# Carry stationary, weights moving: a two-way row scan with its product turned by VectorE

## What is computed

```
v = (x - mean) / sqrt(var + 1e-5)          # per image and group of 32 channels
step(carry, row): new = relu(Wm @ carry + bias) + row      # Wm: 1024 x 1024, row: 1024 x (4*48)
down = scan(step, first row of v, the rows below it)
up   = scan(step, last row of down, the rows of down above it)
out  = x + up
```

## Time and profile before

| | |
|---|---|
| median of 3 runs | 1852.66 us (1851.65 to 1884.84) |
| span of the profiled execution | 1849.8 us |
| mean granted TensorE clock | 0.999 of 2.4 GHz |
| PE busy | 1717.1 us (93%) |
| DVE busy | 1197.4 us (65%) |
| POOL busy | 646.1 us (35%) |
| ACT busy | 316.9 us (17%) |

### The profile page before, as it was taken

The page is one execution under the profiler, slowest core; times in us unless marked ns, Lnnn a source line. Parts: engine busy times, 40 slices in busy tenths (PEclk is TensorE's granted clock), DMA queues, the critical chain, the costliest instruction groups (busy, mean ns, idle before and its releaser), DMA issues.

```text
span 1849.8 us, 33139 instructions
## 1 busy us (share of the span) xinstructions
PE 1717.1 (93%) x12036; PEld 1716.1 (93%) x12036; DVE 1197.4 (65%) x3282; ACT 316.9 (17%) x763; POOL 646.1 (35%) x1145
## 2 busy tenths in 40 slices
PE   0029999999999999999999999999999999999999
PEld 0029999999999999999999999999999999999999
DVE  7998666666666666666665666556565656566564
ACT  0011111111111111111111111111111111111111
POOL 0046444445444444444432222222222222222222
PEclk9999999999999999999999999999999999999999
DMA  9953222121212222220002242424333333424111
GB/s 352 368 188 120 95 76 102 68 103 68 102 68 103 76 94 87 83 97 23 0 0 78 110 153 102 153 102 154 115 140 124 132 134 122 147 108 153 51 51 51
DMA packets 61436, 206.07 MB, mean 111 GB/s; under 512 B 4160, under 2 KB 33856, under 8 KB 61376
## 3 DMA queue, kind: packets, MB, share of 16 engines
q1 hardware_dynamic: 61232, 205.54, 30.9%
q10 hardware_dynamic: 144, 0.00, 0.0%
HBM read 136.32 MB, written 69.21 MB: 111 GB/s over the span
## 4 chain that ended last, share of the span: by engine, by line
PE 91%; DMA 4%; DVE 4%; SPq 1%; issue 0%; ACT 0%; POOLq 0%; POOL 0%; DVEq 0%
PE bank L411 63%; PE bank L413 28%; DMA x_ring<-x_rows 2%; DMA d_ring<-x_rows 2%; DVE work L286 1%; SPq L142 1%; DVE d_ring L342 1%; DVE moments L297 0%; DVE carry L332 0%; DVE carry L334 0%; DVE w_lo L349 0%; DVE d_ring L365 0%; DVE summed L360 0%; DVE spread L311 0%; ACT work L273 0%
## 5 line engine op out<-in xcount | busy, mean ns | idle before, releaser
L411 PE MATMUL bank<-carry,w_hi 128*128 128x384 f32 x6016 | 1715.6, 360 | 13.2 <-DVE carry L334 10.0
L413 PE MATMUL bank<-carry,w_lo 128*128 128x192 f32 x6016 | 1507.6, 251 | 0.0
L413 PEld LDWEIGHTS bank<-carry,w_lo 128*128 128x128 f32 x6016 | 1151.2, 191 | 0.0
L411 PEld LDWEIGHTS bank<-carry,w_hi 128*128 128x128 f32 x6016 | 1131.1, 188 | 13.9 <-issue 9.9
L360 DVE TENSOR_TENSOR summed<-bank,work 128x192 f32<-128x192 f32 x752 | 267.0, 355 | 552.6 <-ACT work L273 531.9
L273 ACT ACTIVATE work<-bank,bias_sb 128x192 f32<-128x192 f32 x752 | 307.4, 421 | 1416.2 <-PE bank L413 1416.2
L243 POOL TENSOR_TENSOR x_ring<-x_ring,d_ring 128x192 f32<-128x192 f32 x384 | 228.8, 596 | 662.6 <-DVE carry L334 649.9
L334 DVE TENSOR_TENSOR carry<-d_ring,carry 128x192 fp32r<-128x192 f32 x752 | 337.7, 449 | 26.2
L223 POOL TENSOR_TENSOR xn<-x_ring,gn_mean 128x192 f32<-128x192 f32 x376 | 214.9, 572 | 396.2 <-DVE d_ring L365 387.1
L332 DVE CAST carry<-d_ring 128x192 fp32r<-128x192 f32 x752 | 197.2, 262 | 26.1
L226 POOL TENSOR_TENSOR xn<-xn,gn_rstd 128x192 f32<-128x192 f32 x376 | 191.5, 509 | 29.5
(11 more groups left out here) (24 smaller groups left out, 12.2 us busy)
## 6 DMA issues: line engine op xcount, KB each, us to landing
x_ring<-x_rows SPq DMA_DIRECT2D x88, 768.0 KB, 6.9
out_rows<-x_ring SPq DMA_DIRECT2D x47, 768.0 KB, 3.9
down_rows<-d_ring SPq DMA_DIRECT2D x40, 768.0 KB, 3.6
d_ring<-down_rows SPq DMA_DIRECT2D x40, 768.0 KB, 5.7
d_ring<-x_rows SPq DMA_DIRECT2D x12, 1536.0 KB, 16.2
x_ring<-x_rows SPq DMA_DIRECT2D x8, 1536.0 KB, 16.4
d_ring<-w_t SPq DMA_DIRECT2D x7, 512.0 KB, 8.9
out_rows<-x_ring SPq DMA_DIRECT2D x8, 96.0 KB, 1.6
```

The source lines that it names most:

```text
L411: pe.matmul(bank[m][:, 0:2 * COLS], w_hi[:, k, out_cols], carry[:, parity, k, :, :].rearrange("p s c -> p (s c)"), start=(k == 0), stop=False)
L413: last = pe.matmul(bank[m][:, 0:COLS], w_lo[:, k, out_cols], carry[:, parity, k, 0, :], start=False, stop=(k == K - 1))
```

## The change

The operands change places: 128 columns of the carry are the stationary operand, and 512 columns of the weights (half of the output channels) are the moving one. A row of 192 columns (4 images by 48) is cut into three chunks of 64 columns (4 images by 16). The three chunks are independent chains. A "step" `i` is now one chunk of one row, 282 in all (3 chunks, 94 rows). Job `j` computes one half of the output channels, half `j % 2`, for the two steps `j-1` and `j`, whose 64 columns each lie side by side as 128 stationary columns. So a step gets one of its halves in job `i` and the other in job `i+1`. There are 283 jobs; the first and the last have one step. Each has 24 matmuls of 512 columns, into one bank (8 tiles `k`, three part products).

The product now stands in PSUM with the carry's columns on the partitions and the output channels along a row, and it has to be turned before it can be the next carry. DVE does this with 16 transposes a job (`turn_blocks`, L442): each reads 32 partitions (quadrant `q`) by 128 elements of the bank and writes 32 partitions (quadrant `u`) of the buffer `turn`. The weights' output channels are laid out by the host so that this gives whole tiles. After the 16th, `direct_done` is raised; ACT does four activations in place (relu with bias, L341), raises `rectified`, and DVE makes two halves of rows from it (L457: product plus row, 128 by 256 elements each). ACT rounds each half to `st_hi` (L347), and POOL takes the remainder to `st_lo` (L289). Job `j` reads, in its first 12 matmuls, halves that job `j-3` completed, and in its last 12 also the half that job `j-2` completed.

```
-            def product(parity, m, k):
-                pe.matmul(bank[m][:, 0:2 * COLS], w_hi[:, k, out_cols], carry[...hi and lo...])
-                pe.matmul(bank[m][:, 0:COLS], w_lo[:, k, out_cols], carry[:, parity, k, 0, :])
+            for j in range(JOBS):
+                if j >= BANKS:
+                    pe.wait_ge(direct_done, j - BANKS + 1)
+                for n in range(K):
+                    k = KB * blocks_of(j)[n // KB] + n % KB
+                    wait_split(hi_ready, first_hi, j, n)
+                    pe.matmul(out, stationary(st_hi, j, k), w_cols(w_hi, o, k), ...)
+                    pe.matmul(out, stationary(st_hi, j, k), w_cols(w_lo, o, k), ...)
+                    wait_split(lo_ready, first_lo, j, n)
+                    last = pe.matmul(out, stationary(st_lo, j, k), w_cols(w_hi, o, k), ...)
+                    if final:
+                        last.then_inc(acc_ready, 1)
+            def turn_blocks(j):
+                dve.wait_ge(acc_ready, j + 1)
+                if j >= 2:
+                    dve.wait_ge(y_ready, first_done(j - 2))
+                for u in range(QUADS):
+                    for q in range(used(j) // B32):
+                        final = dve.transpose(target(j, q, u), source(bank[j % BANKS], q, u))
+                final.then_inc(direct_done, 1)
+            def make_half(j, i):
+                ... waits for xn_ready and d_stored (down) or d_loaded (up) ...
+                dve.tensor_tensor(here, product_of(j, i), addend, ALU.add).then_inc(y_ready, 1)
+            for j in range(JOBS):
+                turn_blocks(j)
+                dve.wait_ge(rectified, j + 1)
+                for i in members(j):
+                    make_half(j, i)
+            def rectify(j):                                     # ACT
+                act.wait_ge(direct_done, j + 1)
+                for kk in range(KB):
+                    cols = channels[j % 2][:, kk, 0:used(j)]
+                    final = act.activation(cols, cols, ACT.Relu, bias=bias_sb[:, k:k + 1])
+                final.then_inc(rectified, 1)
```

More of the change, by code:

```diff
@@ L26, with row_of, blocks_of, first_done @@
 P = 128
-SLOTS = 8
+K = 8
+KB = 4
+C = 1024
+H = 48
+NI = 4
+WIDTH = 48
+COLS = NI * WIDTH
+CHUNKS = 3
+W16 = WIDTH // CHUNKS
+Q = 64
+HALF = 512
+B32 = 32
+QUADS = 4
 GN_GROUP = 32
 GN_EPS = 1e-5
+BN_DIM = 6
+RING = 8
+GROUPS = H // RING
+LAST = GROUPS - 1
 STAT_CHUNKS = 4
-DVE_LO = 3
-WAVE = 5
-BN_DIM = 6
-def build(nc, x_rows, w_t, bias, down_rows, out_rows):
[L37 to L48, removed]
+TC = K // STAT_CHUNKS
+ROWS = H - 1
+STEPS = CHUNKS * ROWS * 2
+DOWN = CHUNKS * ROWS
+JOBS = STEPS + 1
+XN_SLOTS = 4
+BANKS = 8
+W_TILES = 16
+W_POOL = 13
+XN_AHEAD = 2
+SLOT_AT = ((0, 0), (0, 1), (P, 1), (P, 0))
+PAIR_AT = ((0, 2), (0, 1), (1, 2), (P, 1))
+def row_of(i):
+    step = i // CHUNKS
+    return step + 1 if step < ROWS else 2 * ROWS - 1 - step
+def blocks_of(j):
+    return ((j + 1) % 2, j % 2)
+def first_done(i):
+    return 2 * i + 1
+def second_done(i):
+    return 2 * i + 2
+def members(j):
+    return [i for i in (j - 1, j) if 0 <= i < STEPS]
+def build(nc, x_rows, w_t, bias, down_rows, out_rows):
     with ExitStack() as ctx:
@@ L58, in build @@
         w_lo = sb("w_lo", [P, K, C], F32R)
[L59 to L64, removed]
+        st_hi = sb("st_hi", [P, K, 2 * P], F32R)
+        st_lo = sb("st_lo", [P, K, 2 * P], F32R)
+        x_ring = sb("x_ring", [P, RING, K * COLS])
+        d_ring = sb("d_ring", [P, RING, K * COLS])
+        xn = sb("xn", [P, XN_SLOTS, K * Q])
+        turn = sb("turn", [P, 3 * HALF])
         bias_sb = sb("bias_sb", [P, K])
@@ new lines, in build, with w_place, w_order, w_cols @@
+        w_raw = [raw_area[:, t * HALF:(t + 1) * HALF] for t in range(W_TILES)]
+        def w_place(t):
+            o, n = divmod(t, K)
+            return o, KB * blocks_of(o)[n // KB] + n % KB
+        def w_order(o, k):
+            b = blocks_of(o).index(k // KB)
+            return K * o + KB * b + k % KB
+        def w_cols(w, o, k):
+            return w[:, k, o * HALF:(o + 1) * HALF]
+        def stat_cols(ring, i):
+            return ring[:, :, i * WIDTH:(i + 1) * WIDTH]
+        def x_chunk(h, c, k0=0, k1=K):
+            row = x_ring[:, h % RING, :].rearrange("p (k n w) -> p k n w", k=K, n=NI)
+            return row[:, k0:k1, :, c * W16:(c + 1) * W16]
@@ L165, in _ @@
[L165 to L200, removed]
@@ L228, in _ @@
[L228 to L243, removed]
-                                       ALU.add).then_inc(out_ready, 1)
@@ L268, in _ @@
-            act.wait_ge(bias_loaded, 16)
-            with act.Fori(0, STEPS) as s:
-                for m in range(K):
-                    act.wait_ge(psum_ready, K * s + m + 1)
-                    act.activation(act_part[:, m, :], bank[m][:, COLS:2 * COLS], ACT.Identity,
-                                   bias=bias_sb[:, m:m + 1]).then_inc(act_ready, 1)
+            act.activation(gn_std[:, :], bank[7][:, 0:K * NI], ACT.Sqrt, bias=eps[:, 0:1]).then_inc(std_ready, 1)
+            for t in range(3, K):
+                w_round(t)
@@ new lines, in split_hi @@
+            def split_hi(j, i):
+                b = j % 2
+                act.wait_ge(y_ready, first_done(i) if i == j else second_done(i))
+                act.activation(slot(st_hi, i + CHUNKS, b * KB, (b + 1) * KB),
+                               d_chunk(row_of(i), i % CHUNKS, b * KB, (b + 1) * KB), ACT.Copy).then_inc(hi_ready, 1)
+            for j in range(JOBS):
+                rectify(j)
+                for i in members(j):
+                    if i < STEPS - CHUNKS:
+                        split_hi(j, i)
@@ new lines, in wait_split @@
+            def wait_split(ready, first, j, n):
+                if j == 0 and n in (0, KB):
+                    pe.wait_ge(first, 1 + n // KB)
+                elif j in (1, 2) and n == 0:
+                    pe.wait_ge(first, 2 + j)
+                elif j >= CHUNKS and j < STEPS:
+                    if n == 0:
+                        pe.wait_ge(ready, first_done(j - CHUNKS))
+                    elif n == KB:
+                        pe.wait_ge(ready, second_done(j - CHUNKS))
+            for j in range(JOBS):
+                o = j % 2
+                out = bank[j % BANKS][0:used(j), :]
+                if j >= BANKS:
+                    pe.wait_ge(direct_done, j - BANKS + 1)
+                for n in range(K):
+                    k = KB * blocks_of(j)[n // KB] + n % KB
+                    final = n == K - 1
+                    wait_split(hi_ready, first_hi, j, n)
+                    if j < 2:
+                        wait_w(w_hi_ready, None, o, k)
+                    pe.matmul(out, stationary(st_hi, j, k), w_cols(w_hi, o, k), start=(n == 0), stop=False)
+                    if j < 2:
+                        wait_w(w_lo_ready, w_lo_rest_ready, o, k)
+                    pe.matmul(out, stationary(st_hi, j, k), w_cols(w_lo, o, k), start=False, stop=False)
+                    wait_split(lo_ready, first_lo, j, n)
+                    last = pe.matmul(out, stationary(st_lo, j, k), w_cols(w_hi, o, k), start=False, stop=final)
+                    if final:
+                        last.then_inc(acc_ready, 1)
```

363 lines of the change are left out of this document (184 added, 179 removed).

## The result

The changed kernel takes 2217.88 us (median of 4 runs, 2217.83 to 2218.11), and is slower by 19.75%: the ratio is 1.1975, 95% interval 1.1954 to 1.1996. Two of the runs of before taken beside it were disturbed (1885 us); the ratio leaves them out. The forecast was 2253 us.

What follows compares the result with a forecast made beforehand. PE bounded the kernel before; DVE was to bound the changed one: 281 cycles of 7.50 us plus 142.4 us for the ends make 2250, with 2.9 from profiled span to median 2253 us; range 1815 to 2480.

Steps and rivals of the forecast that it cites:

- PE's side: PE's matmuls: 5.12 to 5.66 us a job, 1449 to 1602 us for all 283, a gain on offer of 114 to 267.
- The sum of DVE: DVE's cycle for a job, a plain sum of transposes, wait for ACT and additions: 7.50 us.
- 16 transposes: DVE's transposes in each job: 0.28 + 0.043 = 0.324 us each, 5.18 us for 16.
- hand to ACT, four activations, hand back: DVE's wait for ACT in each job: 0.05 us there, 1.2 for four activations (1.14 raised), 0.04 back.
- two additions: DVE's additions of 256 elements each, priced from L334 beside POOL: 0.515 us each, 1.03 for two.
- case C: The forecast case, DVE-bound: 2017 us (0.27 a transpose) to about 2500 (0.365, additions at 0.62); chance 0.75.
- The ends: Start and finish of the run: 132.9 us before the whole jobs, 4.3 and 5.2 after, 142.4 us without the cycles.
- The held transposes: DVE's transposes, reading another quadrant each time, follow like the `group_avg` fills: each starts 0.043 us after its forerunner ends.
- A: Rival: DVE's transposes overlap like same-quadrant neighbours, 0.206 us each, cycle 5.70 us, 1747 us, faster by 6%; chance 0.17.
- B: Rival: DVE's transposes have no gap and the lowest price, or part overlap, 0.227 to 0.243 us each; chance 0.05.
- The clock: PE's clock: PE would wait some 2 us a job, and nothing was counted for the clock.
- the other signs: Profile after: DVE near 90% busy or waiting for ACT, chain over DVE and ACT, L442 0.28 us every 0.32.

Runs made afterwards that it cites:

- e1: Changed kernel with all 16 transposes reading and writing from partition 0 on, into a buffer aside, so the product is missing from the result; 1700.91 us.
- e5: Changed kernel without the matmuls with w_lo, 16 instead of 24 a job, their part of the product missing; 2216.12 us.
- e3: Changed kernel with all transpose inputs beginning at partition 0 and outputs as before, a new quadrant every fourth transpose; 1742.57 us.
- e2: Changed kernel with transpose outputs all beginning at partition 0 in a buffer aside, while the input quadrant still changes each time; 2204.4 us.
- e7: Against e6: DVE's 8 copies become transposes straight out of PSUM, ACT keeps its 8 copies, computation complete; 1715.06 us, ratio 0.926 to the kernel before.
- e9: Changed kernel, computation complete, with DVE making the halves of job j-1 after the fifth transpose of job j; 1848.28 us, ratio 0.9979 to the kernel before.
- e6: Changed kernel, computation complete, with one long transpose into a buffer, then 16 quadrant copies, 8 on ACT, 8 on DVE; 2021.46 us, ratio 1.0913 to before.
- e8: Against e6: POOL's two normalising passes and sum with x touch 16 elements instead of 512, its splits kept; 1699.5 us.

## Why the prediction was right

**PE's side.** Forecast 5.12 to 5.66 us a job, measured some 5.53: a matmul starts every 0.230 us in e1, where PE hardly ever waits (5651 of them between 300 and 1600 us), and every 0.231 or 0.232 in the changed kernel. The loss between two matmuls did not go away with their size: some 0.2305 us against 0.213 of streaming, 17 ns, against 22 ns before. (The 0.213 is an estimate, one column a clock period at 2.4 GHz; at 1.2 GHz e5 shows a start every 0.428 us, 512 periods.) At the PE bound the kernel would take 1701 us (e1), so the offer was real, 152 us, within the 114 to 267 stated.

**The sum of DVE.** Forecast 7.50 us, measured 7.35. By its terms:

| term | forecast us | measured us |
|---|---|---|
| 16 transposes | 5.18 (0.28 + 0.043 each) | 5.21 (0.312 + 0.014 each) |
| hand to ACT, four activations, hand back | 0.05 + 1.2 + 0.04 | 1.35 (the activations 1.29) |
| two additions | 1.03 | 0.76 + 0.03 |

The price of a transpose is right to 1%, but by two errors that cancel: the instruction is 0.03 us longer than the copy it was scaled from, and the gap behind it 0.03 us shorter than behind a fill. The same instruction lasts 261 ns in e1, where it is not held. The 0.365 us at the upper end of case C counts 32 elements more, a term that no run shows; the changed kernel starts a transpose every 0.3265 us, and none of its 4512 lasts over 0.325. Nor does a row show the 0.06 us by which ACT's 1.14 was raised for reading SBUF; the four took 1.29.

The additions were mis-sized. I had priced them by L334, 449 ns for 192 elements next to a busy POOL. Here POOL is waiting for the splits that follow the additions (idle for 3.75 us up to 1008.79, the additions run from 1007.82 to 1008.58), and they are shorter: 0.42 us for 256 elements, the second overlapping the first. The row that was needed was in the trace of before, where L334 also runs with POOL idle (for 9.10 us up to 143.61):

```profile
138.21 0.36 DVE L334 TENSOR_TENSOR carry<-d_ring,carry 128x192 fp32r<-128x192 f32 x1
```

0.36 us and 64 elements more at 1.04 ns are 0.43, as measured. The error is 0.24 us a job, 67 us in all. It is more than the whole of what the forecast was too high (35 us); the transposes and the wait for ACT, each a little longer than forecast, took 25 of it back, and the start 8.

**The ends.** 132.9 us was forecast for the start of job 1's transposes; it was 141.3. The timeline of DVE in the changed kernel shows why:

```profile
123.58 0.68 DVE L411 TENSOR_TENSOR d_ring<-x_ring,gn_mean 128x512 f32<-128x512 f32 x1
...
130.99 4.71 DVE L432 TENSOR_TENSOR w_lo<-d_ring,w_hi 128x512 fp32r<-128x512 f32 x3
135.62 1.55 DVE L418 TENSOR_TENSOR st_lo<-d_ring,st_hi 128x512 fp32r<-128x512 f32 x1
137.09 2.55 DVE L442 STREAM_TRANSPOSE turn<-bank 32x128 f32<-32x128 f32 x8
```

I had counted POOL's pieces and took DVE's own for done. With POOL at work beside them (the weights, then the first rows), DVE's remainders of 512 elements take some 1.6 us each; the subtraction of the same size at 123.58, which starts while POOL is idle (122.00 to 123.79), takes 0.68. So DVE reaches job 0 at 137.1, and job 0's own half cycle (4.2 us) comes on top. This cost 8.4 us, and with the cycle's -0.15 x 281 = -42 us it makes all but a microsecond of the difference of -35.

**The held transposes.** The forecast took the price of a held transpose from four fills at the head of the program, which change only their output quadrant. The transposes change theirs with every fourth only; what they change every time is the input's, and for that no row of before spoke. Carrying the fills over was a step without a row behind it, and e3 shows what it was worth: with the outputs alone the time is 1743 us. The runs supply what was missing: a start every 0.20 us without a change of quadrant (e1), 0.323 with a change of input quadrants alone (e2), and three held transposes of 16 with the outputs alone (e3).

**The rivals.** A (overlapping transposes, 1747 us) is what e1 and e3 made of the kernel: 1701 and 1743. Its price of 0.206 us was right to 3%; only its condition does not hold in the changed kernel. B, a part overlap, did not come about either: no transpose there lasts less than 0.297 us, and one starts every 0.3265. Of C's upper reach nothing came about, for the reason given on the additions. The clock stayed up (0.997), as counted, with PE waiting 1.8 us a job (forecast some 2). PE's busy share is 78%, not the 70 named as a sign; the other signs came as forecast.

## To carry to other kernels

When an operand order is changed for TensorE's sake, add up what the turned result costs on the engine that turns it, its waits included, and compare that sum, job by job, with TensorE's: here TensorE's side offered 152 us, and the turning put 517 on top of that (1701 to 2218), so that 365 were lost. An instruction's price has to come from a row with the same neighbours beside it (L334 of before, 192 elements: 0.54 us beside POOL at 132.98, 0.36 without it at 138.21). Many short VectorE instructions that alternate between quadrants did not overlap here (0.312 us each, a start every 0.3265); doing the bulk in one long instruction (0.72 us) and dividing the quadrant moves over two engines made the kernel faster than both (e7, 1715 us). And where a helper engine answers in the middle of another's list, put work between question and answer (e9: 370 us for a change of order).

## What the hardware showed that was not expected

- A transpose of 32 by 128 f32 elements out of PSUM on DVE lasted 0.261 us, and one started every 0.20, when all began in one quadrant (e1). With the input quadrant changing each time it lasted 0.31 and one started every 0.323 us (e2), with the output quadrant changing every fourth time as well every 0.3265 (changed kernel). One of 128 by 512 elements, sixteen times the data, lasted 0.72 us (e7).
- ACT's relu passes of 128 elements over all partitions overlapped: four of 0.39 us took 1.28 (e7), a start every 0.30. Its quadrant copies did not: 0.309 us long, eight took 2.55 us (e6, e7), a start every 0.32. Whether the quadrant is the cause on ACT was not tried.
- DVE's copies from SBUF to SBUF took longer beside POOL's long passes (e6: 0.223 us in the median, up to 1.244; eight 4.17 us against 2.35 in e8), and its subtractions with two SBUF inputs took 1.6 us for 512 elements beside POOL at the start of the changed kernel, against 0.68 for the one that began with POOL idle. Its transposes out of PSUM did not: with POOL busy 40% of the changed kernel's span none of the 4512 lasted over 0.325 us.
- TensorE lost 17 ns between matmuls of 512 columns, hardly less than the 22 between those of 384 and 192. Where the clock was granted at 1.2 GHz nothing was seen of it: in e5 seven such matmuls start from 1003.01 to 1005.58, one every 0.428 us, and 512 columns at 1.2 GHz are 0.427. What the loss is was not tried.
- In e5, with 16 matmuls a job in the same cycle of 7.35 us and 1.93 us of waiting before a job in the mean, TensorE's clock was granted at 1.2 GHz for part of a job (1003 to 1006 us), after the job had begun at 2.4; in the changed kernel, with 24 matmuls and 1.2 us of waiting before each job, its mean was 0.997 of 2.4 GHz. The wait in front of the job did not decide it alone: the clock also fell in e5's job at 1008.12, which has 1.21 us of waiting before it (six matmuls start from 1009.94 to 1012.08, one every 0.428 us). What decides it was not tried.
